# Attention over paged keys and values: own keys in blocks of four heads, division after the product with the output weights' input, low parts on VectorE, value pages spread over the partitions

## What is computed

```python
q, k, v = x @ Wq.T, x @ Wk.T, x @ Wv.T        # 32 query heads, 8 key heads of 128
q, k = rope(rmsnorm(q, q_norm_w), pos), rope(rmsnorm(k, k_norm_w), pos)
kc = k_cache[block_table]                     # 16 pages of 32 keys: 512 cached keys per sequence
vc = v_cache[block_table]
k_all, v_all = concat(kc, k), concat(vc, v)   # 512 cached + 32 own keys = 544
scores = q @ k_all.T * 128 ** -0.5            # cached keys from cache_seqlens on are masked
o = softmax(scores) @ v_all
x = x + o @ Wo.T
```

## Time and profile before

| | before |
|---|---|
| median of 3 runs | 2888.45 us (2887.26 to 2891.68) |
| span of the profiled execution | 2886.1 us |
| TensorE busy (products) | 2721.6 us, 94% |
| VectorE busy | 2042.3 us, 71% |
| ScalarE busy | 1441.0 us, 50% |
| GpSimd busy | 1352.4 us, 47% |
| moved by DMA | 507.06 MB, 176 GB/s over the span |
| attention | about 1006 to 2511 us of the span |
| output projection | about 2516 to 2886 us of the span |

### The profile page before, as it was taken

The page is one execution under the profiler, slowest core; times in us unless marked ns, Lnnn a source line. Parts: engine busy times, 40 slices in busy tenths (PEclk is TensorE's granted clock), DMA queues, the critical chain, the costliest instruction groups (busy, mean ns, idle before and its releaser), DMA issues. The chain is left out here.

```text
span 2886.1 us, 58057 instructions
## 1 busy us (share of the span) xinstructions
PE 2721.6 (94%) x16646; PEld 2298.8 (80%) x16647; DVE 2042.3 (71%) x3956; ACT 1441.0 (50%) x2637; POOL 1352.4 (47%) x1008
## 2 busy tenths in 40 slices
PE   7699899999999589999999999999999999799999
PEld 5587677777777478888888888888888888778887
DVE  5355339999999678888888888888888888542221
ACT  3222234444444366666666666666666666431111
POOL 1222165665565555566666666555666666200000
PEclk9899899999999799999999999999999999999999
DMA  6422432332332488887778888888877888353332
GB/s 221 128 76 69 159 109 89 92 102 84 89 89 77 146 248 237 243 237 229 231 237 236 237 234 237 240 236 242 237 229 231 237 236 236 110 208 117 137 109 84
DMA packets 364201, 507.06 MB, mean 176 GB/s; under 512 B 56547, under 2 KB 269731, under 8 KB 360292
## 3 DMA queue, kind: packets, MB, share of 16 engines
q1 hardware_dynamic: 336036, 416.54, 49.2%
q0 software_dynamic: 25984, 86.79, 8.7%
q10 hardware_dynamic: 2112, 2.89, 0.3%
HBM read 407.98 MB, written 98.04 MB: 175 GB/s over the span
## 5 line engine op out<-in xcount | busy, mean ns | idle before, releaser
L1303 POOL TENSOR_TENSOR att_k_lo<-att_k_raw,att_k_hi 128x1024 fp32r<-128x1024 f32 x256 | 606.0, 2367 | 502.4 <-ACT att_k_hi L1337 502.3
L1395 DVE TENSOR_SCALAR att_prob<-att_prob,att_inv_total 128x544 f32<-128x544 f32 x512 | 635.8, 1242 | 0.0
L1329 ACT ACTIVATE att_pt<-att_ps_pt 128x512 f32<-128x512 f32 x512 | 305.8, 597 | 497.6 <-PE att_ps_s L1476 497.6
L1488 PE MATMUL att_ps_o<-att_pt,att_v 128*128 128x128 f32 x4096 | 541.2, 275 | 0.0
L1488 PEld LDWEIGHTS att_ps_o<-att_pt,att_v 128*128 128x128 f32 x4096 | 497.9, 192 | 6.4
L884 POOL TENSOR_TENSOR qkv_part_b<-qkv_normed,qkv_cross 128x256 f32<-128x256 f32 x320 | 297.6, 951 | 240.3 <-DVE qkv_normed L1044 240.3
L1322 ACT ACTIVATE att_prob<-att_prob,att_shift 128x544 f32<-128x544 f32 x512 | 378.4, 739 | 0.0
L76 PE MATMUL att_ps_s<-att_k_hi,att_q_hi 128*128 128x272 f32 x1024 | 349.1, 341 | 26.5 <-POOL att_k_lo L1303 26.1
L1383 DVE CUSTOM_DVE_ANT_0 att_prob<-att_ps_s,att_mask 128x544 f32<-128x544 f32 x512 | 360.2, 704 | 2.2 <-PE att_ps_s L78 2.2
L1473 PE MATMUL att_ps_pt<-att_ident,att_prob 128*128 128x128 f32 x2048 | 318.6, 278 | 23.0 <-DVE att_prob L1395 12.4
L76 PE MATMUL qkv_ps_y<-qkv_w_hi,qkv_xt_hi 128*128 128x512 f32 x768 | 320.2, 417 | 0.0
(11 more groups left out here) (174 smaller groups left out, 4893.5 us busy)
## 6 DMA issues: line engine op xcount, KB each, us to landing
att_k_raw<-in_k_pages SPq DMA_DIRECT2D x1024, 128.0 KB, 3.9
att_v<-in_v_pages SPq DMA_DIRECT2D x1024, 128.0 KB, 3.1
q_t<-qkv_out_t SPq DMA_DIRECT2D x128, 256.0 KB, 2.3
att_q_raw<-q_t POOLq DMA_DIRECT2D x64, 512.0 KB, 4.1
o_t<-att_o POOLq DMA_DIRECT2D x64, 512.0 KB, 6.2
out_o<-o_t SPq DMA_DIRECT2D x32, 1024.0 KB, 6.5
qkv_w_stage<-in_w_qkv SPq DMA_DIRECT2D x12, 1024.0 KB, 5.2
l_w_stage<-in_w SPq DMA_DIRECT2D x8, 1024.0 KB, 7.0
```

The costliest lines, as they stand in the source:

```text
L1303: pool.tensor_tensor(lo, raw, f32(hi), ALU.subtract).then_inc(pool_split, 1)
L1329: act.activation(pt_sb[:, j % 2, :, :], ps_pt[:, j % 2, :, :], ACT.Copy).then_inc(pt_ready, 1)
L1395: dve.tensor_scalar(prob[:, b, :], prob[:, b, :], inv_total[:, b:b + 1], None, ALU.mult)\
L1488: pe.matmul(out, v_sb[:, p, c, h * DH:(h + 1) * DH], pt_sb[:, j % 2, c, :], start=(c == 0), stop=False)
```

## The change

It redoes the attention in five parts.

1. **Own keys in blocks.** VectorE copies each unit's probabilities of the 32 own keys to `p_own` (`gather`). Every fourth unit TensorE turns the four of them as one 128x128 block into `spare(1, P)`, and VectorE's `copy_own` brings it to SBUF once for the four. The own values lie in `vo_sb` with 128 rows for each unit: its own 32 rows at the unit's place, and zeros elsewhere (set once), so the product with the block gives the unit's part. The own values are loaded by four transfers instead of one.
2. **Division moved.** The exponentials are not divided. Their sums stay for a sequence in `total`, are turned by TensorE after its eighth unit into `spare(0, HK)`, inverted by VectorE (`invert`) and stored to DRAM (`inv_t`). `output_projection` loads them, spread over all partitions (`load_inv`), and multiplies each half of the outputs by them (`scale`) ahead of the high part. Its weights get two staging buffers instead of three.
3. **Low parts on VectorE.** All six are made by `split_lo` there, at the units in `LO_AT`. GpSimd only issues transfers.
4. **Order.** TensorE does `scores(u+2)`, `outputs(u-4)`, `transpose(u)`, with four buffers of transposed probabilities; ScalarE does the exponential ahead of the copy.
5. **Value pages spread.** Page n of a block of four goes to every fourth partition, from n on. So that the keys have the same order, the high and low parts of the keys are written with their pages interleaved (`(k n)` instead of `(n k)`), and the array of key numbers that the mask is made from is reordered in the same way.

```diff
 
...
+HI_AT = [(5,), (2,), (3,), (4,), (), (), (0,), (1,)]
+LO_AT = [(1,), (5,), (2,), (3,), (4,), (), (), (0,)]
...
 PIECE_TURN = {c: n + 1 for n, c in enumerate(EARLY_PIECES + LATE_PIECES)}
...
         k_hi, k_lo = m.sb("k_hi", [P, 2, HK, NALL], fp32r), m.sb("k_lo", [P, 2, HK, NALL], fp32r)
...
-        v_sb, vo_sb = m.sb("v", [P, 2, NPP // 4, HK * DH]), m.sb("vo", [SEQ, 2, HK * DH])
...
-        o_sb = m.sb("o", [P, 2, HK, P])
+        prob, p_own = m.sb("prob", [P, NB_P, NALL]), m.sb("p_own", [P, 2, OG, SEQ])
+        shift, total = m.sb("shift", [P, NB_P]), m.sb("total", [P, 2, HK])
+        pt_sb, pto_sb = m.sb("pt", [P, OG, NKEY // P, P]), m.sb("pto", [P, 2, P])
...
-                    *(b[:, p, :, first * PSIZE:(first + n) * PSIZE].rearrange("p h (n k) -> p n h k", n=n)
+                    *(b[:, p, :, first * PSIZE:(first + n) * PSIZE].rearrange("p h (k n) -> p n h k", n=n)
...
+        def spare(half, rows):
+
+            return ps_s[0:rows, 1, half, D - P:D]
...
-                                sp.wait_ge(pool_split, ON_POOL * (s - 2) + c + 1)
+                                sp.wait_ge(lo_done, PIECES * (s - 2) + PIECE_TURN[c])
...
                 def load_v(s, p, pages):
+
                     if later(s, 2):
                         sp.wait_ge(pv_done, HK * (s - 1))
...
-                        at = (n % 4) * PSIZE
-                        sp.dma_start(v_sb[at:at + PSIZE, p, n // 4, :], v_pages[bass.ds(page, 1)])\
+                        sp.dma_start(v_sb[n % PPP:P:PPP, p, n // PPP, :], v_pages[bass.ds(page, 1)])\
                           .then_inc(v_loaded[p], 16)
...
-                    pool.dma_start(vo_sb[:, p, :], v_own[bass.ds(s * SEQ, SEQ), :]).then_inc(own_v_loaded[p], 16)
+                    rows = v_own[bass.ds(s * SEQ, SEQ), :].rearrange("k (g u d) -> k g u d", g=HK // OG, u=OG)
+                    for u in range(OG):
+                        pool.dma_start(vo_sb[u * SEQ:(u + 1) * SEQ, p, :, u, :], rows[:, :, u, :])\
+                            .then_inc(own_v_loaded[p], 16)
...
+                    pool.wait_ge(inv_ready, s + 1)
+                    pool.dma_start(inv_t[bass.ds(s, 1)].rearrange("s (h q) -> (s h) q", h=HK), inv_sb[:, p, :])\
+                        .then_inc(inv_stored[p], 16)
...
-                        for c in range(ON_POOL):
-                            raw, hi, lo = piece(c, p)
-                            pool.wait_ge(hi_done, PIECES * s + PIECE_TURN[c])
-                            pool.tensor_tensor(lo, raw, f32(hi), ALU.subtract).then_inc(pool_split, 1)
+                        load_own_v(s, p)
...
-                                   accum_out=total[:, b:b + 1]).then_inc(exp_done, 1)
+                                   accum_out=total[:, j // HK, j % HK:j % HK + 1]).then_inc(exp_done, 1)
...
-                    if later(u, 2):
-                        act.wait_ge(pv_done, u - 1)
-                    act.activation(pt_sb[:, j % 2, :, :], ps_pt[:, j % 2, :, :], ACT.Copy).then_inc(pt_ready, 1)
+                    if later(u, OG):
+                        act.wait_ge(pv_done, u - OG + 1)
+                    act.activation(pt_sb[:, j % OG, :, :], ps_pt[:, j % 2, :, :], ACT.Copy).then_inc(pt_ready, 1)
...
-                        copy_pt(u, j)
                         if not (last and j >= UNITS - 2):
                             exponential(u + 2, (j + 2) % UNITS)
+                        copy_pt(u, j)
...
-                            for c in PIECES_AT[j % HK]:
+                            for c in HI_AT[j % HK]:
                                 split_hi(2 * i + ahead, i + ahead // 2 + 1, ahead % 2, c)
...
+                def gather(u, j):
+
+                    dve.wait_ge(exp_done, u + 1)
+                    dve.tensor_copy(p_own[:, j // OG % 2, j % OG, :], prob[:, j % NB_P, NKEY:NALL]).then_inc(gathered, 1)
...
-                def invert(u, j):
-                    dve.wait_ge(exp_done, u + 1)
-                    dve.reciprocal(inv_total[:, j % 4:j % 4 + 1], total[:, j % 4:j % 4 + 1]).then_inc(inverted, 1)
-
-                def normalise(u, j):
-                    b = j % 4
-                    dve.wait_ge(inverted, u + 1)
-                    dve.tensor_scalar(prob[:, b, :], prob[:, b, :], inv_total[:, b:b + 1], None, ALU.mult)\
-                       .then_inc(normed, 1)
-
-                def copy_own(u, j):
-                    dve.wait_ge(t_done, u + 1)
-                    if later(u, 2):
-                        dve.wait_ge(pv_done, u - 1)
-                    dve.tensor_copy(pto_sb[:, j % 2, :], ps_s[0:SEQ, (j + 1) % 2, 1, D - P:D]).then_inc(pto_ready, 1)
-
-                def copy_o(i, u, j):
-
-                    p, g = j // HK, j // OG
-                    dve.wait_ge(pv_done, u + 1)
-                    if later(u, UNITS):
+                def copy_own(i, g):
+
+                    dve.wait_ge(t_done, UNITS * i + OG * (g + 1))
+                    if later(i, 1) or g >= 2:
+                        dve.wait_ge(pv_done, UNITS * i + OG * (g - 1))
+                    dve.tensor_copy(pto_sb[:, g % 2, :], spare(1, P)).then_inc(pto_ready, 1)
...
+                def invert(i, p):
+
+                    dve.wait_ge(t_done, UNITS * i + HK * (p + 1))
+                    if later(i, 1):
+                        dve.wait_ge(inv_stored[p], 16 * i)
+                    dve.reciprocal(inv_sb[:, p, :], spare(0, HK)).then_inc(inv_ready, 1)
...
-                    dve.tensor_tensor(lo, raw, f32(hi), ALU.subtract).then_inc(dve_split, 1)
-
-                for c in range(ON_POOL, PIECES):
+                    dve.tensor_tensor(lo, raw, f32(hi), ALU.subtract).then_inc(lo_done, 1)
...
+                for c in PIECE_TURN:
                     split_lo(0, 0, c)
+                for c in LO_AT[HK - 1]:
+                    split_lo(1, 1, c)
...
                 def pair(i, last):
                     for j in range(UNITS):
-                        u = UNITS * i + j
+                        u, s, p = UNITS * i + j, 2 * i + j // HK, j // HK
+                        if j % OG == 0 and later(u, OG):
+                            copy_own(*group_before(i, j, 1))
+                            if j % HK == 0:
+                                invert(*group_before(i, j, 1)[:1], (1 - p))
                         if not (last and j >= UNITS - 2):
                             wait_for_scores(2 * i + (j + 2) // HK, u + 2, (j + 2) % UNITS)
                         if not (last and j >= UNITS - 1):
-                            invert(u + 1, j + 1)
+                            gather(u + 1, (j + 1) % UNITS)
                         if not (last and j >= UNITS - 2):
                             mask_and_max(u + 2, (j + 2) % UNITS)
-                        copy_own(u, j)
-                        if not (last and j >= UNITS - 1):
-                            normalise(u + 1, j + 1)
-                        if not (last and j >= HK):
-                            for c in DVE_PIECES_AT[j % HK]:
-                                split_lo(2 * i + j // HK + 1, 1 - j // HK, c)
-                        if j % OG == 1:
-                            if j > 1:
-                                copy_o(i, u - 2, j - 2)
-                            elif later(u, UNITS):
-                                copy_o(i - 1, u - 2, UNITS - 1)
+                        if not (last and j >= HK - 1):
+                            ahead = 2 if j % HK == HK - 1 else 1
+                            for c in LO_AT[j % HK]:
+                                split_lo(s + ahead, (p + ahead) % 2, c)
+                        if j % OG == 1 and later(u, 2 * OG):
+                            copy_o(*group_before(i, j, 2))
...
-                        copy_o(i, UNITS * i + UNITS - 1, UNITS - 1)
+                        copy_own(i, UNITS // OG - 1)
+                        invert(i, 1)
+                        copy_o(i, UNITS // OG - 2)
+                        copy_o(i, UNITS // OG - 1)
...
-                        pe.wait_ge(pool_split, ON_POOL * (2 * i + p + 1))
-                        pe.wait_ge(dve_split, (PIECES - ON_POOL) * (2 * i + p + 1))
+                        pe.wait_ge(lo_done, PIECES * (2 * i + p + 1))
                     if later(u, 2):
                         pe.wait_ge(masked, u - 1)
-                    if later(u, 3):
-                        pe.wait_ge(pto_ready, u - 2)
+                    if j % OG == 3 and later(u, OG + 3):
+                        pe.wait_ge(pto_ready, UNITS // OG * i + j // OG)
+                    if h == 3 and later(u, HK + 3):
+                        pe.wait_ge(inv_ready, 2 * i + p)
...
-                def transpose(u, j):
-                    pe.wait_ge(normed, u + 1)
+                def transpose(u, j, last):
+                    p, g = j // HK, j // OG
+                    pe.wait_ge(exp_done, u + 1)
                     if later(u, 2):
                         pe.wait_ge(pt_ready, u - 1)
                     for c in range(NKEY // P):
```

(60 more changed lines are left out.)

70 lines of the change are left out of this document (40 added, 30 removed).

## The result

The changed kernel takes 2966.87 us (median of 4 runs, 2964.47 to 2967.72); the kernel before, run beside it, takes 2889.25 us. The ratio is 1.0266, with an interval of 1.0251 to 1.0281. The prediction was 2694.5 us, with a range of 2660 to 2820: wrong in size and in sign. The profiled execution has a span of 2966.1 us against 2886.1, so 80.0 us have to be found.

A forecast was written before the change was run, and what follows sets the result against it. TensorE was taken as the attention's bound, 2.81 of 2.927 us a head, falling to 2.52 with slips. 2886.1 - 208 (attention) - 2 (start) + 1 + 1 (end) + 14 (output stage) = 2692.1, median 2694.5 us, range 2660 to 2820.

The forecast's parts named there:

- Step (b): TensorE, attention: the two own-value records on 128 rows instead of 32 take 0.245 us, saving 0.175 us a head.
- Step (c): TensorE's new order: the first score product's extra 0.10 us goes, or half of it, saving 0.05 to 0.10 us a head.
- Rival D: TensorE, own values: the 0.27 us isn't from the 32 rows, so 2.74 us a head, median 2817 us; chance 0.1.
- ScalarE's work doesn't change: ScalarE, attention: 2.31 us a head as before, under TensorE's 2.50, heaviest heads 2.58 by durations.
- rival A: High and low parts with one element every 16 bytes are slower: a head about 2.70 us, median 2787 us; chance 0.2.
- Rival B: Slower than before: scattered read and write each add a stream, low part 3.4 us, median 3073 us; chance 0.07.
- Slack 0.7, zero: TensorE, each group's fourth transpose: the mask two heads ahead takes 1.7 us, asked for at 2.4, so no cost.
- it fits with 0.7 us to spare: SP's queue: 19.3 us of work for 32 page loads within the new sequence of 20.0 us.
- rival C: Transfers set the pace: spread pages gain nothing or SP's issuing takes longer; 2.69 us a head, median 2781; chance 0.1.
- hidden: Attention's transfers: if spread value pages reach the keys' rate, the need is 275 of about 315 GB/s, no cost.
- Start: -2: Before the first scores: the last low part is done earlier on VectorE than on GpSimd, -2 us (0 to -4).
- Output stage: +14: Output stage: +6 for inverse sums' load and multiplication, the rest for two weight buffers; bounds +5 and +25.

The follow-up runs named there:

- e9: Changed kernel with plain keys, value pages still spread, and 8 of 16 V pages per sequence issued by GpSimd instead of SyncE: 2628.35 us.
- e7: Kernel of e1 with the own-value product back on 32 rows instead of 128: 2804.35 us.
- e6: Changed kernel with VectorE making each low part one head later, two heads behind the high part: 2874.91 us.
- e1: Changed kernel without its fifth part, value pages in 32 neighbouring partitions and keys written without gaps: 2654.98 us.
- e2: Changed kernel with keys written without gaps, value pages still spread: 2807.35 us.
- e3: Changed kernel with value pages back in neighbouring partitions, keys still interleaved: 2967.39 us.
- e14: Kernel of e1 with 8 of 16 plain V pages per sequence issued by GpSimd: 2678.71 us (2650.80 to 2691.84).
- e8: Kernel of e1 without the output stage's division, inverse sums neither loaded nor multiplied: 2636.51 us.
- e10: Kernel of e1 as a bench, each piece of cached keys copied and subtracted in another access pattern: 2900.85 us, a single run.
- e4: Kernel before with the fifth part alone, value pages spread and key parts interleaved, GpSimd still making low parts: 2958.21 us.
- e13: Changed kernel with pages interleaved by twos instead of fours, and 8 of 16 V pages per sequence issued by GpSimd: 2633.15 us.

## Why the prediction was wrong, point by point

**The bound of before, and TensorE's steps.** Right, and too careful in the sum. The division's removal and the 128-row products gave TensorE a pace of its own of 2.346 us (e9, busy 200 of 200), where I had 2.50. Step by step in its clean head: scores 0.84 (taken as 0.76 to 0.81), cached values 0.89 (0.98 kept), own values 0.22 (0.245), transposes 0.35 (0.44). With the 0.05 us of the transposes of own keys and row sums (0.04 forecast) that is 2.346. Step (b) was mis-sized: 32 rows cost 0.35 us in e7, not 0.225 to 0.275, since they also delay what comes ahead of them, which I hadn't counted. Step (c), which charged 0.44 for transposes with the turn to a product from the qkv stage, overcharged by 0.09, and took the first product's extra 0.10 for a cost of the 32 rows that would go. It stayed: in the changed kernel the second product starts 0.21 us behind the first (1703.31 to 1703.52), the others 0.12 to 0.13 apart, with 128 rows everywhere. Rival D fell: 32-row records do cost what they look like.

**VectorE and ScalarE: the step that failed.** The low parts of 1024 columns at 1226 ns each, and "ScalarE's work doesn't change", were false for the four pieces of cached keys: 2055 and 2068 ns. I had two bounds, named the pattern as rival A, and gave the forecast the contiguous end because the nearest rows in shape had it. A row that is near in shape but has another access pattern bounds nothing; no row of before had the pattern, and with the penalty that the prediction itself took from the Trainium skill (Advanced Engine Details and Errata, SBUF Cachelines), the middle between the ends should have been the forecast, or A the likeliest.

**But rival A's own time was wrong as well.** It foresaw the prices (up to 2.37 and 1.9 us; measured 2.055 and 2.068, ScalarE's a little over its bound) and gave 2787 us, because it divided the engines' work by eight heads: 2.6 and 2.84 us a head at most, 2.70 taken. (It also counted five slower pieces, "5/8", where the change has four: the queries stay together, at 1049 and 1222 ns.) The real head is 3.00 with neither engine full. The pieces stand in some heads only, each high part behind a mask's exponential and each low part ahead of the next mask, and these lines chain up over three heads (8.83 us in the timeline). e6 shows that the order counts and not only the amount of work: the same instructions, of nearly the same length, moved by a head, give 84 us back between the first and the last mask. It doesn't show that the whole loss is the chain's, since e6 got a new wait and stays at 2.836 us. Rival B (3073 us) had the sign right and the mechanism wrong: it wanted a low part of over 2.9 us, where 2.06 was enough.

**TensorE's new waits: "Slack 0.7, zero".** The working was right for a low part of 1.2 us: in e1 and e9, L1505's counterpart doesn't hold TensorE between 1500 and 2200 us. With 0.83 us more for the low part and 1.0 for the high part the 0.7 were gone, and this is where TensorE stands, 2.3 us once a sequence. I had the slack's size beside rival A's price and didn't put the two together.

**SP: "it fits with 0.7 us to spare".** Wrong. It charged spread V pages like the old ones, though the change edits the very instruction that SP issues. In e2 a page takes 0.66 us to issue instead of 0.52 as in e1, 2.2 us more per sequence, and the head is 2.690: rival C's number (2.69) by its second cause, "SP's issuing takes longer", while its first (spread pages gain nothing) is refuted by e9. So even with free interleaving the change would have taken 2807 us.

**DMA: "hidden".** Right in direction and wrong in what follows. The like pair is the changed kernel and e3, both with a head of 3.00 us: spread value pages land in 3.0 us with the transfers at a share of 0.72 for 227 GB/s, neighbouring ones in 3.7 us at 0.81 for 230. The Trainium skill (SBUF — State Buffer, section on the DMA port swizzle) says that partitions 0 to 31 reach 8 of the 16 ports and all 128 reach 16; the pair agrees in direction. But at TensorE's real pace plain pages are not hidden: e1 has transfers busy all the time and 2.385 us, e9 2.346. From e1 to e9 (2654.98 to 2628.35, 27 us) the second queue came too; by itself it gained nothing (e14, 2650.80 at best), so spreading is worth at least 22 us there.

**Start: -2, measured +13.8.** The first mask now has a low part of the second sequence ahead of it on VectorE, whose pages have only begun to arrive. The timeline of VectorE in the changed kernel:

```profile
1018.95 1.99 DVE L1436 TENSOR_TENSOR att_k_lo<-att_k_raw,att_k_hi 128x1024 fp32r<-128x1024 f32 x1 [10.09 <-ACT att_k_hi L1354]
...
1021.37 0.72 DVE L1405 CUSTOM_DVE_ANT_0 att_prob<-att_ps_s,att_mask 128x544 f32<-128x544 f32 x1
```

It stands 10.09 us for the high part, makes the low part at 1018.95, and only then the first mask. I had gone through what the first scores wait for, not through what is queued ahead of the first mask. e6 has nothing there and its first mask comes 10.0 us earlier.

**End: +2, measured +5.8.** The 18.7 us from the last mask to the stage's first load are 18.7 in e1 too, so the interleaving has no part in them; what makes them up stays open.

**Output stage: +14 with bounds 5 and 25, measured +22.3.** The first product:

```profile
2590.86 0.77 PE L76 MATMUL out_ps_y<-out_w_hi,out_o_hi 128*128 128x512 f32 x1 [26.44 <-DVE out_w_lo L1646]
```

It starts 17.0 us behind the stage's first load (2573.87), where it was 2528.14 - 2516.2 = 11.9: +5.1 where I had +6. What is larger comes behind it. Three steps of VectorE up to the first tile's addition:

```profile
2604.21 2.29 DVE L1653 TENSOR_TENSOR out_o<-out_o,out_inv 128x2048 f32<-128x2048 f32 x1 [1.46 <-DMA out_inv<-inv_t]
...
2627.63 2.29 DVE L1653 TENSOR_TENSOR out_o<-out_o,out_inv 128x2048 f32<-128x2048 f32 x1 [1.85 <-DMA out_inv<-inv_t]
...
2634.11 0.68 DVE L1666 TENSOR_TENSOR out_y<-out_ps_y,out_x 128x512 f32<-128x512 f32 x1
```

The addition comes at 2634.11, 60.2 us into the stage; before, 39.9. Of the +14 the division had 6 and the weight buffers 8; e8 has 13.9 for the division and leaves 7.4 with the buffers. So it is the division's term that was mis-sized. By the timeline, what I missed of it is that the multiplication of the next tile stands on VectorE ahead of that addition (2627.63), and that of the tile's second half (2604.21) ahead of the last four groups of weights. The 15 tiles after the first take 2963.0 - 2634.1 = 328.9 us against 2883.0 - 2556.1 = 326.9: the zero that I gave them was 2.0.

**The sum.** 512 x (3.00 - 2.52) = 246 us of the miss are in attention; 16 at the start, 4 at the end and 8 in the output stage make 274, and 2966.1 - 2692.1 is 274.0.

## What to carry to other kernels

A change of layout is paid by every instruction that walks it, so each of them has to be priced in the new pattern, the queue that issues its transfers included, and a row of the old pattern is no price for it. Where two engines hand pieces to each other within one ring, don't divide their work by the number of heads: write down the chain through the heaviest heads, and compare it with the slack of each new wait. Where the full step of a layout is what costs, try half of it: here it kept the parts fast, and the kernel was as fast within 5 us as the one with spread pages and plain keys, though with less room left on the transfers.

## What the runs showed of the hardware

- ScalarE, VectorE and GpSimd on 1024 float32 elements per partition: 1049, 1222 and 2367 ns together; 2068, 2055 and 3008 ns with a step of 16 bytes. A step of 8 bytes: 1127 and 1208 on ScalarE and VectorE. It doesn't matter whether the operand with the step is read or written, nor how many have it (e10 for ScalarE and VectorE; GpSimd was seen in e4 alone, with one input and the output in steps).
- SyncE issues a 128 KB page into 32 neighbouring partitions in 0.52 us (e1) and into every fourth partition in 0.66 (e2). At the same pace the spread page lands sooner: 3.0 us (changed kernel) against 3.7 (e3). Every second partition costs like every fourth: 8 in 5.07 us (e13).
- A pair of 32-row records among 128-row ones costs 0.35 us more than a pair of 128-row ones: 0.19 itself, 0.09 ahead of it, 0.07 behind (e7 against e9).
- Behind 2.31 us of standing still TensorE's granted clock was 0.52 for 3 us and its products took 0.43 us instead of 0.29; from 1716 us on it was 1.00 again (changed kernel).
- In the kernel before with part 5 (e4), VectorE's division takes 746 ns on average, with GpSimd subtracting for 3008 ns at a time with a step, where it took 1242 beside GpSimd's contiguous 2367. Half of them take 483 ns or less in e4, where the median was 1382, though the longest is longer (2877 against 1931). GpSimd in that pattern disturbs VectorE less; why, no run here tells.
